# Scattering each slot's results to token rows during the slot loop, and reading them back with plain transfers

## The reference

```
logits = flat @ router_w.T                       # 592 x 8
probs = softmax(logits)
topk_probs, topk_idx = top_k(probs, 2)
importance = probs.sum(axis=0)
running = 1 + 0.1 * (importance - 1) + 0.01
balanced = topk_probs / running[topk_idx]
balanced = balanced / balanced.sum(-1)
outs = (silu(flat @ w1[e].T)) @ w2[e].T          # for every expert e: 192 -> 512 -> 192
combined = (outs[topk_idx] * balanced).sum()     # each token's two experts
h = h + combined
```

## Time and profile before

| | |
|---|---|
| median of 3 runs | 233.69 us (232.89 to 236.68) |
| the profiled execution | 231.64 us, of which the span from first to last instruction is 229.9 us |
| mean granted clock of TensorE | 0.867 of full |
| busy: TensorE matmul / VectorE / ScalarE / GpSimd | 83% / 47% / 22% / 32% of the span |
| chain that ended last | TensorE 54%, DMA 13%, GpSimd 13%, VectorE 11% |

### The profile page before, as it was taken

One profiled execution on the slowest core, in us unless ns is written; L12 is line 12 of the kernel. 1 busy time (PEld: TensorE's weight loads), 2 busy tenths in 40 slices (PEclk: granted clock), 3 DMA queues, 4 the chain that ended last, 5 costly groups with the idle time before them and its releaser, 6 DMA issues.

```text
span 229.9 us, 2843 instructions
## 1 busy us (share of the span) xinstructions
PE 191.1 (83%) x910; PEld 133.4 (58%) x910; DVE 108.3 (47%) x301; ACT 50.4 (22%) x118; POOL 73.5 (32%) x77
## 2 busy tenths in 40 slices
PE   0199982899572999479999799898999999999990
PEld 0199740476232645238477468545686777789990
DVE  3222771093849755945477877043131323213173
ACT  2000011049440313211232107111212212121100
POOL 1474499100008927812360727000000000000771
PEclk9999996599975559955579999959999999999997
DMA  6999999999766992000000101233201010111242
GB/s 222 424 426 312 329 371 331 264 252 250 192 145 132 358 347 74 0 3 0 0 0 1 43 21 61 60 87 88 69 17 34 20 34 17 37 34 34 69 123 63
DMA packets 24734, 30.71 MB, mean 134 GB/s; under 512 B 2015, under 2 KB 21260, under 8 KB 24720
## 3 DMA queue, kind: packets, MB, share of 16 engines
q1 hardware_dynamic: 22720, 25.50, 37.7%
q10 hardware_dynamic: 1008, 3.28, 3.8%
q0 software_dynamic: 992, 1.76, 2.8%
HBM read 18.46 MB, written 12.31 MB: 134 GB/s over the span
## 4 chain that ended last, share of the span: by engine, by line
PE 54%; DMA 13%; POOL 13%; DVE 11%; issue 5%; ACT 1%; SPq 1%; POOLq 0%; DVEq 0%
PE ps L1072 13%; PE ps L1092 9%; PE ps L804 6%; PE ps L868 5%; PE ps L889 5%; DMA vrows<-vn 4%; POOL early L365 4%; PE ps L850 4%; PE ps L1084 3%; DMA early<-in_patch_w 3%; POOL xn L336 2%; DMA v<-vrows 2%; PE ps L877 2%; PE ps L1056 2%; POOL vw L348 2%
## 5 line engine op out<-in xcount | busy, mean ns | idle before, releaser
L348 POOL TENSOR_TENSOR vw<-v,wm 111x768 f32<-111x768 f32 x16 | 29.8, 1887 | 49.5 <-DMA v<-vrows 28.4
L365 POOL DMA_INDIRECT early<-yrows,sidx x10 | 9.7, 969 | 71.4 <-DMA yrows<-early 68.7
L1072 PE MATMUL ps<-w1s,early 96*128 x60 | 31.0, 645 | 0.7 <-DVE early L784 0.7
L784 DVE COPY early<-ps 96x256 f32<-96x256 f32 x15 | 6.3, 421 | 42.3 <-PE ps L1056 42.3
L804 PE MATMUL ps<-early 128*128 128x192 f32 x80 | 15.6, 362 | 10.6 <-DVE early L547 10.6
L889 PE MATMUL ps<-vw,pt 111*64 111x192 f32 x128 | 17.4, 433 | 5.9 <-POOL vw L348 5.8
L1092 PE MATMUL ps<-w2s,early 128*128 x120 | 21.8, 326 | 0.0
L804 PEld LDWEIGHTS ps<-early 128*128 128x128 f32 x80 | 15.2, 216 | 10.7 <-issue 10.6
L1092 PEld LDWEIGHTS ps<-w2s,early 128*128 128x128 f32 x120 | 19.2, 190 | 0.0
L868 PE MATMUL ps<-early,qt 97*64 97x444 f32 (+1 forms) x64 | 18.8, 726 | 0.3 <-ACT qt L407 0.3
L1072 PEld LDWEIGHTS ps<-w1s,early 96*128 96x128 f32 x60 | 12.0, 208 | 10.6 <-issue 10.6
(11 more groups left out here) (142 smaller groups left out, 274.0 us busy)
## 6 DMA issues: line engine op xcount, KB each, us to landing
yrows<-zero SPq DMA_DIRECT2D x1, 4416.0 KB, 16.1
xrows<-zero SPq DMA_DIRECT2D x1, 4320.0 KB, 30.8
early<-in_patch_w SPq DMA_DIRECT2D x4, 960.0 KB, 11.7
w1s<-in_w SPq DMA_DIRECT2D x8, 384.0 KB, 14.7
w2s<-in_w SPq DMA_DIRECT2D x8, 384.0 KB, 14.1
early<-in_pixels ACTq DMA_DIRECT2D x4, 640.0 KB, 11.9
early<-xrows SPq DMA_DIRECT2D x15, 96.0 KB, 1.9
yrows<-early SPq DMA_DIRECT2D x15, 96.0 KB, 1.6
```

What stands on the lines that cost most here:

```text
L348: nc.gpsimd.tensor_tensor(vw[:, j % 2, a, :, :], v3[:, 2 * j + a, :].unsqueeze(1).to_broadcast([CHK, GQ, C]), wm[:, :, :], ALU.mult).then_ ...
L365: nc.gpsimd.indirect_dma_start(out=yg[:, i, k, :], out_offset=None, in_=yrows, in_offset=bass.IndirectOffsetOnAxis(ap=sidx[:, k, i:i + 1], ...
L1072: m = nc.tensor.matmul(ps[:, s % 2, :], xgt[0:HC, s % 3, c, :], w1s[:, bass.ds(expert[s], 1), c, :].rearrange("p a n -> p (a n)"), start=( ...
```

## The change

The results are scattered, slot by slot, straight to the row of their token and choice, so that the reading at the end is plain.

- The row of `xrows` grows from 192 to 193 numbers (CW). The 193rd is the number of the token and choice to which it belongs, 640 x choice + token, which comes as ten new columns of the constants. Cleared rows hold NOID = 2560 there, which is out of bounds. The clearing of `xrows`, the scatters to it and the loads of `xg` are of 193-number rows (772 bytes in place of 768).
- Before the scatters GpSimd waits for the last scores (the new buffer `xid` lies in `early`), copies the ten numbers into `xid`, and for each tile copies `xn` twice (once for each choice) into `xid`. The copies of a group stand ahead of the group's scatters and behind those of the group before.
- In the slot loop GpSimd converts each slot's numbers to integers (`sid`) and, when the result is in `yo`, scatters it to `yrows`, which has one row for each choice and token (1,280 rows in place of 5,888). SyncE's 15 stores to `yrows` and the ten gathers are gone.
- SyncE waits for all scatters and reads `yg` with one plain DMA for each tile (two rows for each token). The last tile's routed shares take 80 rows.

```diff
+CW = C + 1
+NOID = 4 * TP
...
-        xrows = nc.dram_tensor("xrows", (NOROW, C), F32, kind="Internal").ap()
+        xrows = nc.dram_tensor("xrows", (NOROW, CW), F32, kind="Internal").ap()
...
-        yrows = nc.dram_tensor("yrows", (NOROW + P, C), F32, kind="Internal").ap()
+        yrows = nc.dram_tensor("yrows", (TOPK * TP, C), F32, kind="Internal").ap()
...
-            for t in range(SLOTS):
-                sp.wait_ge(y_ready, t + 1)
-                sp.dma_start(yrows[bass.ds(row[t], P), :], yo[:, t % 4, :]).then_inc(y_out[t % 4], 16)
+            for i in range(TILES):
+                n = P if i < TILES - 1 else TAIL
+                for b in range(4):
+                    sp.wait_ge(y_out[b], 16 * len(range(b, SLOTS, 4)))
+                sp.dma_start(yg[0:n, i, :, :], yrows.rearrange("(k t) n -> t k n", k=TOPK)[P * i:P * i + n]).then_inc(back[i], 16)
...
             pool.wait_ge(cleared, 32)
+            pool.wait_ge(ld_rt, 64)
+            pool.wait_ge(s_done, PAIRS)
+            nc.gpsimd.tensor_copy(xid[:, :, :, C:CW], ids).then_inc(id_set, 1)
+            pool.wait_ge(id_set, 1)
             for g, (tiles, _) in enumerate(PLACED):
+                for i in tiles:
+                    pool.wait_ge(x2_ready, i + 1)
+                    nc.gpsimd.tensor_copy(xid[:, i, :, 0:C], xn[:, i, :].unsqueeze(1).to_broadcast([P, TOPK, C])).then_inc(row_made, 1)
+                pool.wait_ge(row_made, tiles[-1] + 1)
                 pool.wait_ge(idx_ready, g + 1)
...
-                            in_=xn[:, i, :], in_offset=None, bounds_check=SPARE - 1, oob_is_err=False).then_inc(scattered, 16)
-
+                            in_=xid[:, i, k, :], in_offset=None, bounds_check=SPARE - 1, oob_is_err=False).then_inc(scattered, 16)
+
+            for t in range(SLOTS):
+                pool.wait_ge(ld_g[t], 16)
+                nc.gpsimd.tensor_copy(sid[:, t:t + 1], xg[:, t, C:CW]).then_inc(sid_ready, 1)
+                pool.wait_ge(sid_ready, t + 1)
+                pool.wait_ge(y_ready, t + 1)
+                nc.gpsimd.indirect_dma_start(
+                    out=yrows, out_offset=bass.IndirectOffsetOnAxis(ap=sid[:, t:t + 1], axis=0),
+                    in_=yo[:, t % 4, :], in_offset=None, bounds_check=TOPK * TP - 1, oob_is_err=False).then_inc(y_out[t % 4], 16)
             for b in range(4):
                 pool.wait_ge(y_out[b], 16 * len(range(b, SLOTS, 4)))
-            for i in range(TILES):
-                for k in range(TOPK):
-                    nc.gpsimd.indirect_dma_start(
-                        out=yg[:, i, k, :], out_offset=None, in_=yrows,
-                        in_offset=bass.IndirectOffsetOnAxis(ap=sidx[:, k, i:i + 1], axis=0)).then_inc(back[i], 16)
...
-                dve.wait_ge(back[i], 16 * TOPK)
+                dve.wait_ge(back[i], 16)
```

More of the change, by code:

```diff
@@ L87, in build @@
         gt = part(2 * IC * T).rearrange("p (b i t) -> p b i t", b=2, i=IC)
-        yg = part(TILES * TOPK * C).rearrange("p (i k n) -> p i k n", i=TILES, k=TOPK)
-        xg = part(SLOTS * C).rearrange("p (s n) -> p s n", s=SLOTS)
+        sent = part(TILES * TOPK * CW)
+        xid = sent.rearrange("p (i k n) -> p i k n", i=TILES, k=TOPK)
+        yg = sent[:, 0:TILES * TOPK * C].rearrange("p (i k n) -> p i k n", i=TILES, k=TOPK)
+        xg = part(SLOTS * CW).rearrange("p (s n) -> p s n", s=SLOTS)
         xgt = part(3 * 2 * P).rearrange("p (b c t) -> p b c t", b=3, c=2)
@@ L117, in build @@
         steps, slot_no, first_row, spare_row, region, iot = cuts[3:9]
-        zero = sb("zero", [P, C])
+        ids = cuts[9].rearrange("p (i k o) -> p i k o", i=TILES, o=1)
+        zero = sb("zero", [P, CW])
+        sid = sb("sid", [P, SLOTS], U32)
         w1s = sb("w1s", [HC, EXPERTS, 2, INNER])
@@ L198, in build @@
         xn_ready = sem("xn_ready")
+        id_set = sem("id_set")
+        row_made = sem("row_made")
+        sid_ready = sem("sid_ready")
         xnt_ps = sem("xnt_ps")
@@ L278, in _ @@
             sp.dma_start(con[:, :], consts).then_inc(ld_rt, 16)
-            sp.wait_ge(zero_set, 1)
+            sp.wait_ge(zero_set, 2)
             sp.dma_start(xrows.rearrange("(s p) n -> p s n", p=P),
-                         zero[:, :].unsqueeze(1).to_broadcast([P, NOROW // P, C])).then_inc(cleared, 16)
+                         zero[:, :].unsqueeze(1).to_broadcast([P, NOROW // P, CW])).then_inc(cleared, 16)
             for e in EXPERT_ORDER:
@@ L298, in _ @@
             sp.dma_start(yrows.rearrange("(s p) n -> p s n", p=P),
-                         zero[:, :].unsqueeze(1).to_broadcast([P, NOROW // P + 1, C])).then_inc(cleared, 16)
+                         zero[:, 0:C].unsqueeze(1).to_broadcast([P, TOPK * TILES, C])).then_inc(cleared, 16)
             sp.wait_ge(rows_ready, 1)
@@ L320, in _ @@
             pool.wait_ge(ones_set, 1)
-            nc.gpsimd.memset(zero[:, :], 0.0).then_inc(zero_set, 1)
+            nc.gpsimd.memset(zero[:, 0:C], 0.0).then_inc(zero_set, 1)
+            nc.gpsimd.memset(zero[:, C:CW], float(NOID)).then_inc(zero_set, 1)
             nc.gpsimd.memset(half[:, :], -0.5).then_inc(half_set, 1)
@@ L770, in routed_share @@
             def routed_share(i):
-                dve.wait_ge(back[i], 16 * TOPK)
+                dve.wait_ge(back[i], 16)
+                rows = P if i < TILES - 1 else TAIL
                 for k in range(TOPK):
-                    ins = nc.vector.scalar_tensor_tensor(out=h[:, i, :], in0=yg[:, i, k, :], scalar=wk[:, k, i:i + 1],
-                                                         in1=h[:, i, :], op0=ALU.mult, op1=ALU.add)
+                    ins = nc.vector.scalar_tensor_tensor(out=h[0:rows, i, :], in0=yg[0:rows, i, k, :], scalar=wk[0:rows, k, i:i + 1],
+                                                         in1=h[0:rows, i, :], op0=ALU.mult, op1=ALU.add)
                     if k < TOPK - 1:
@@ L1124 @@
 EXPERT_ORDER = [FIRST, LAST, *ROUTED]
-CONSTS = [P, TILES * EXPERTS, EXPERTS * EXPERTS, TILES, SLOTS, SLOTS, SLOTS, EXPERTS, EXPERTS]
+CONSTS = [P, TILES * EXPERTS, EXPERTS * EXPERTS, TILES, SLOTS, SLOTS, SLOTS, EXPERTS, EXPERTS, TILES * TOPK]
 CONSTS = tuple(sum(CONSTS[:i + 1]) for i in range(len(CONSTS)))
@@ L1190 @@
         rows(np.tril(np.ones((EXPERTS, EXPERTS))), P * np.arange(TILES), np.arange(SLOTS), P * np.arange(SLOTS) - REGION,
-             SPARE + P * np.arange(SLOTS), REGION * (np.arange(EXPERTS) - ROUTED[0]), np.arange(EXPERTS))], axis=1)
+             SPARE + P * np.arange(SLOTS), REGION * (np.arange(EXPERTS) - ROUTED[0]), np.arange(EXPERTS)),
+        np.arange(TOPK * TP, dtype=np.float32).reshape(TOPK, TILES, P).transpose(2, 1, 0).reshape(P, -1)], axis=1)
     w_w = f(L0_attn_w_w)
```

2 lines of the change are left out of this document (removed).

## The result

| | before | changed |
|---|---|---|
| median | 234.56 us (4 runs, 232.89 to 236.68) | 242.32 us (4 runs, 240.82 to 243.18) |
| profiled execution, span | 231.64 us, 229.9 us | 243.18 us, 241.4 us |

The changed kernel is slower: ratio 1.0349, 95% interval 1.025 to 1.0448. It lies 7 us above the forecast of 235.2 and 4 above the end of its range.

A forecast was written before the change was run, and what follows sets the result against it. Bound by the scatters to `xrows`, TensorE alone from 147 to 209, then two chains (gathers, TensorE) ending almost together. Terms -2.4 + 1.3 + 0.4 + 1.25 + 0.95 = +1.5 on 233.69 gave 235.2 us, range 231.4 to 238.4.

The forecast's parts named there:

- Part 6: Clearing `xrows` with 772-byte rows, ahead of weights and `vrows` store: 8% longer, 0.95 us cost, between 0 and 19%.
- The rival of dear rows: Clearing ahead of the weights: unaligned rows cost 19% more, 2.3 us, giving +2.85, 236.5 us; chance 0.14.
- Part 1: Kernel's tail: plain reads replace the gathers and hide behind TensorE's last work; gain 2.4 us.
- Part 2: Slot loop: each slot's number copy and scatter fit within a slot of 3.45 us; cost 0.
- Part 3: Copies for tiles 0 and 1, after GpSimd's last `vw`: they block VectorE's `mark(0)` and norm; cost 1.3 us.
- Part 4: Copies for tiles 2 and 3, before the second group's `sidx`: they block VectorE in `mark(1)`; cost 0.4 us (0 to 1.0).
- Part 5: Copy for tile 4, between second and third groups' scatters: nothing hides it; cost 1.25 us (0.8 to 1.6).
- The clock: TensorE's 1.2 GHz stretch after its wait before the first slot might shift either way: 0 in sum, 1.5 us in range; chance 0.06.

The follow-up runs named there:

- e2: Kernel before, with the clearing ahead of the weights going to an unused DRAM tensor of 772-byte rows and `xrows` cleared behind the values; 240.98 us.
- e16: Changed kernel with `xrows` cleared behind the values and the copy of tile 4 made ahead of the second group's scatters; median 222.94 us, ratio 0.947.
- e4: Changed kernel with the clearing of `xrows` moved behind the values; median 222.33 us, ratio 0.9709 to the kernel before.
- e6: Kernel before with the clearing of `xrows` (768-byte rows) moved behind the values; median 224.78 us, ratio 0.9686.
- e14: Changed kernel with the clearing of `xrows` moved behind the values, run again on another chip; median 223.90 us, ratio 0.9562 to the kernel before.
- e15: Kernel before with the clearing of `xrows` moved behind the values, run again on another chip; median 226.21 us, ratio 0.9614.
- e7: Changed kernel with rows of 832 bytes in place of 772, clearing still ahead of the weights; median 232.66 us, ratio 1.0032 to the kernel before.

## Why the prediction was wrong, point by point

**Part 6 failed**, the clearing with rows of 772 bytes. I took 8%, 0.95 us, with 19%, 2.3 us, as the upper end; it measured +10.8 us of landing in the change and +9.7 by itself in e2, and it passed on to the first `vw`, as the part said it would. The place and the chain were right (all weights and the `vrows` store stand behind it, at a full DMA share), and so was the nothing for the other odd rows (the last scatter takes 2.22 us against 2.23, an `xg` load 1.9 in both); the price of the clearing was short by a factor of eleven. The rival of dear rows named this place and this sign, with a chance of 0.14, and had its size from the same rule. The error was to let the only rule at hand be the end of the range. No row of the trace showed a write off a multiple of 32 bytes, so the upper bound was unknown and should have been open; I named half the rate, 12 us, in a subordinate clause of the rival and left it out of the range. With a term on the chain of 12.1 us at full pace, any factor on it decides the sign. The sum also had no term for slower weights behind the clearing, 3.3 us of the profiled pair, whose cause is open.

**Part 1**, the tail: forecast 2.4, measured 14.0 - 11.5 = 2.4 us (unrounded 13.97 - 11.55). The reads landed later than I reckoned (2.5 to 4.4 us each, where I allowed 3) and it made no difference, as said.

**Part 2**, the scatters in the loop at nothing: right. GpSimd waits for the result ahead of nearly every scatter, mostly 2.5 us; `yo` never held up ScalarE.

**Part 3**, copies of tiles 0 and 1: forecast 1.3, measured 0.4 (14.3 - 13.9). A copy takes 0.48 and not 0.65, and it held up only two of the small instructions, for 0.22 each; the blocking is real, but an instruction of VectorE slips in between two of GpSimd. **Part 4** forecast 0.4; the copies met the norm of tile 4 and not `mark(1)`, and two instructions beside them took 0.5 and 0.1 longer. The delay grew by 1.4 us there (14.3 to 15.7), but how much of that is blocking can't be read off, because TensorE's clock fell at the same time. **Part 5** forecast 1.25, measured 2.39 - 1.29 = 1.10 us; e16 takes it away. Parts 3 to 5 together were forecast at 2.95 us, and TensorE's first slot came 3.0 later than the first `vw` accounts for (16.9 - 13.9). The pairs with the late clearing, where the first `vw` starts within 0.3 us, say the same: e4's first slot starts 3.2 us after e6's (141.95 and 138.76), e14's 3.4 after e15's (142.41 and 138.97).

**The clock**: I left it at nothing with 1.5 us for the range. The low stretch came at the same time as before, 148.3 to 155.1 us before and 148.5 to 155.3 after, but it met other work: before, the first slot's matmuls (eight of line 1072 in 6.36 us), after, the dense matmuls ahead of the last scatters, which then ran twice as long (eight of line 1008 in 5.41 against 2.83 us), while the same eight slot matmuls took 3.70. The short matmuls of `rank(1)` took 0.59 in place of 0.37 us a pair, and VectorE waited 1.27 in place of 0.50 for them, so it delayed the scatters somewhat. It gave 2.7 us back in the slots: TensorE's start of the first slot is 16.9 late and its end 14.0. I had tied the low stretch to TensorE's wait before the first slot, and foretold a wait of 2.4 us; the wait was 0.17, since the slowed dense matmuls filled it, and the low stretch came without it. The eight matmuls of line 1072 in the kernel before (chain), the eight of line 1008 in the changed one (timeline), and two windows of the changed one:

```profile
149.64 6.36 PE ps L1072 x8
```

```profile
150.05 5.41 PE L1008 MATMUL ps<-x2t,w1s 96*128 96x384 f32 x8
```

```profile
150.00:151.00 1.00, 1.00 (x3) 0.70 (x4) 0.58 (x4) 0.00 (x0) 0.00 (x0) 0.50 0.00 0
...
155.00:156.00 1.00, 1.00 (x8) 0.71 (x8) 0.00 (x0) 0.99 (x4) 0.70 (x2) 0.86 0.07 19
```

With 10.8 in place of 0.95 my sum would be +11.35, and the profiled pair differs by 11.5. That is in part luck: 3.3 us of slower weights are not in the sum, and 2.9 came back between TensorE's first slot and its end. Without part 6 the sum is +0.55. e7, which has the clearing at +2.4 in its place, came out 0.7 us above the kernel before, with an interval of half a per cent either way; its other parts thus come to -1.7. So parts 1, 2 and 5 are right one by one, part 3 was 0.9 too high, part 4 can't be read off, and the sum of them all is 2.3 us too high against e7, about what the clock gave back in the profiled pair.

## What to carry to other kernels

Before a row in DRAM is made wider by one number, look at what else is written with that row: here 22.5 KB more cost 10 us in a clearing of 4.3 MB, of which the loads read a third (15 x 128 of 5,760 rows). Round the row up to a multiple of 32 bytes, which left 2.4 us of it here (e7), or keep the aligned row.

A transfer's cost on a full queue is paid by whatever stands behind it. Before pricing it, ask whether it needs to stand there: moving the clearing behind the values gave the kernel before 3 to 4%, more than any part of the change.

Where a price isn't in the trace and the term is large and on the chain, leave the range open by a factor, not by the per cent of a rule.

## What the runs showed of the hardware that I had not expected

- Writes to DRAM of 772 bytes, between 30 and 35 us: 54 to 56 ns for a row and engine when each starts 4 bytes further on than the last, 40 when they start 832 bytes apart; 33 for rows of 768. The share of busy DMA engines is 1.08 to 1.11 in all of them.
- In the same window rows of 772, 800 and 832 bytes cost the same, 40 ns, where they start on multiples of 32. Those of 772 lose 2 us more at the end of their clearing.
- The slow pitch doesn't slow all its rows: the middle one took 45 ns, and one in nine over 100 (e2).
- A scatter of GpSimd that has to wait for a copy starts 0.8 to 0.9 us after it, against 0.30 behind another scatter; the copy itself takes 0.5.
